# Moving the causal mask from TensorE to GpSimd and reordering TensorE's turn in the last stage of a four-block kernel

## The reference

```
log_d = lf[..., 1:, None] - lf[..., None, 1:] + i_pre[..., None, :]
log_d = jnp.where(mask, log_d, -jnp.inf)          # mask: t >= s
m = jnp.max(log_d, axis=-1, keepdims=True)
d_mat = jnp.exp(log_d - m)
s_mat = (q @ k.T) / sqrt(32) * d_mat
denom = max(abs(sum(s_mat)), exp(-m)) + 5e-5
h = s_mat @ v / denom                             # 8 heads of 32
h = h * rsqrt(mean(h * h) + 1e-6) * gain;  x = x + h
gate = softmax(ln(x) @ gate_w.T)                  # 8 experts
t = ln(x) @ lora_U                                # 16 ranks each
x = x + ln(x) @ weight.T + (gate * t) @ lora_V / 16
```

## Time and profile before

| | us |
|---|---|
| median of 3 runs (466.28 to 468.68) | 466.73 |
| the profiled execution | 466.06 |
| its span, first to last instruction | 464.3 |
| PE busy | 357.2 (77%) |
| DVE busy | 347.6 (75%) |
| ACT busy | 246.8 (53%) |
| POOL busy | 214.6 (46%) |
| last stage, from its first log_d to the end | 347.2 to 464.3 |

### The profile page before, as it was taken

The page is one execution under the profiler, slowest core; times in us unless marked ns, Lnnn a source line. Parts: engine busy times, 40 slices in busy tenths (PEclk is TensorE's granted clock), DMA queues, the critical chain, the costliest instruction groups (busy, mean ns, idle before and its releaser), DMA issues.

```text
span 464.3 us, 9131 instructions
## 1 busy us (share of the span) xinstructions
PE 357.2 (77%) x3130; PEld 252.2 (54%) x3137; DVE 347.6 (75%) x998; ACT 246.8 (53%) x454; POOL 214.6 (46%) x215
## 2 busy tenths in 40 slices
PE   3986789998896999434566777657658999999965
PEld 2775567776674777212444444435445666666522
DVE  3887647789999788778999999996243777777751
ACT  1563345654442455444757575757435666666530
POOL 1115001146767463168676767676102555444430
PEclk9998899999996999856878887897958999999985
DMA  7599999966473520000000000000001122222000
GB/s 226 154 259 288 282 339 261 215 145 120 80 146 61 107 32 1 1 0 2 0 0 2 0 1 0 1 1 0 2 0 18 30 47 47 47 47 48 23 24 24
DMA packets 48046, 35.79 MB, mean 77 GB/s; under 512 B 20096, under 2 KB 44032, under 8 KB 47872
## 3 DMA queue, kind: packets, MB, share of 16 engines
q1 hardware_dynamic: 48000, 35.20, 31.6%
HBM read 26.80 MB, written 8.39 MB: 76 GB/s over the span
## 4 chain that ended last, share of the span: by engine, by line
PE 46%; DVE 28%; issue 12%; ACT 5%; DMA 3%; SPq 3%; POOL 1%; DVEq 0%; ACTq 0%
DVE ve L725 6%; PE PS L1436 5%; DVE sm L733 4%; PE PS L1225 3%; PE PS L1214 3%; PE PS L1426 3%; PE PS L1283 3%; PE PS L1244 3%; PE PS L1205 3%; PE PS L1204 3%; PE PS L1403 2%; DVE sm L711 2%; DMA scr_k<-kpart 2%; PE PS L1421 2%; SPq L315 2%
## 5 line engine op out<-in xcount | busy, mean ns | idle before, releaser
L991 ACT ACTIVATE pT<-PS 128x512 f32<-128x512 f32 x64 | 36.5, 596 | 58.6 <-PE PS L1205 58.4
L606 DVE TENSOR_REDUCE negm<-PS 128x4 bf16<-128x512 f32 x64 | 42.3, 683 | 13.3 <-PE PS L1214 13.2
L1318 PE MATMUL PS<-identf,w2f 128*128 128x128 f32 x128 | 23.4, 341 | 36.4 <-ACT w2f L1042 36.4
L469 POOL TENSOR_TENSOR kst<-kst,rows 128x1024 f32<-128x1024 f32 x16 | 37.6, 2349 | 29.6 <-ACT kst L1053 29.6
L453 POOL TENSOR_TENSOR sm<-sm,mhalf 128x1 f32<-128x1 f32 x16 | 11.4, 713 | 81.6 <-DVE sm L638 81.6
L1318 PEld LDWEIGHTS PS<-identf,w2f 128*128 128x128 f32 x128 | 18.3, 174 | 40.8 <-ACT w2f L1042 34.9
L483 POOL TENSOR_TENSOR kst<-kst,rows 128x1024 f32<-128x1024 f32 x16 | 37.7, 2359 | 0.0
L1205 PE MATMUL PS<-identb,negm 128*128 128x128 bf16 x256 | 35.6, 222 | 0.0
L1042 ACT ACTIVATE w2f<-kst,sm 128x1024 f32<-128x1024 f32 x16 | 18.4, 1149 | 31.2 <-DVE sm L741 31.0
L1225 PE MATMUL PS<-pT,vx 128*32 128x128 f32 x512 | 27.7, 291 | 5.0 <-ACT pT L991 4.9
L725 DVE TENSOR_SCALAR ve<-mv 128x2 f32<-128x2 f32 x20 | 30.1, 1504 | 1.8
(11 more groups left out here) (225 smaller groups left out, 1073.2 us busy)
## 6 DMA issues: line engine op xcount, KB each, us to landing
scr_q<-qpart SPq DMA_DIRECT2D x8, 384.0 KB, 5.0
scr_k<-kpart SPq DMA_DIRECT2D x8, 384.0 KB, 6.1
rows<-in_rows SPq DMA_DIRECT2D x1, 2056.0 KB, 11.6
X<-in_x SPq DMA_DIRECT2D x8, 256.0 KB, 4.8
CTXT<-in_ctxT SPq DMA_DIRECT2D x8, 256.0 KB, 4.5
cTb<-in_ctxT SPq DMA_DIRECT2D x16, 128.0 KB, 4.3
vx<-in_ctx SPq DMA_DIRECT2D x16, 128.0 KB, 2.8
out<-rest SPq DMA_DIRECT2D x16, 128.0 KB, 1.7
```

Of the source, the lines that this page charges most:

```text
L469: gp.tensor_tensor(n2[q.slot], n2[q.slot], ln2g, ALU.mult).then_inc(b_g2, 1)
L606: v.tensor_reduce(negm[f.slot % 2][:, 4 * hg:4 * hg + 4], PS[:, 2 + hg % 2, :].rearrange("p (h k) -> p h k", h=4), AX_X, ALU.max, negate=T ...
L991: s.activation(pT[:, hg, :], PS[:, hg % 2, :], ACT.Exp, scale=float(DH0) ** -0.5).then_inc(a_e, 1)
L1318: last = t.transpose(PS[:, 5 + i // 4, (i % 4) * 128:(i % 4 + 1) * 128], u2[:, i * 128:(i + 1) * 128], identf[:])
```

## The change

The mask leaves PE: `maskb` and its matmul go, log_d is one `APARTS` matmul that starts the bank and four `MPARTS` matmuls. In its place POOL runs an `affine_select` in place over each half of `dT` (128 x 512, f32) after ACT's exponential, which writes zero above the diagonal; DVE's weights wait for that (`c_k`) and no longer for the exponential (`c_d`). On POOL the select of half 0 stands behind the gain of `b`, that of half 1 behind L503 and L505 of `c` and ahead of `rr` of `b`.

PE's order becomes: scores (`a`), yT transposes (`b`), nd transposes (`e`), log_d(0), gate transpose (`d`, now into bank 1, columns 256 to 384, waiting for exp(1) of `a` and for the copy `xT` of `e`), values (`a`), experts' product (`d`), log_d(1), products (`e`). The orders of DVE, ACT and SP don't change.

```diff
-            step(gp.memset(maskb[:], 0.0))
-            step(gp.affine_select(out=maskb[:], in_=maskb[:], compare_op=ALU.is_ge, fill=-30000.0, base=0,
-                                  pattern=[[1, 128]], channel_multiplier=-1))
...
+                def masked(half):
+                    pool.wait_ge(c_d, n.b * 2 + half + 1)
+                    d3 = dT[half].rearrange("p (j t) -> p j t", j=4)
+                    gp.affine_select(out=d3, in_=d3, compare_op=ALU.is_ge, fill=0.0, base=0,
+                                     pattern=[[0, 4], [1, 128]], channel_multiplier=-1).then_inc(c_k, 1)
...
+                if n:
+                    masked(0)
                 if c:
                     z = smd[c.slot % 2]
...
+                if n:
+                    masked(1)
                 if b:
                     pool.wait_ge(c_ms, b.b + 1)
...
-                    dve.wait_ge(c_d, a.b * 2 + n + 1)
+                    dve.wait_ge(c_k, a.b * 2 + n + 1)
...
-                    s.activation(gtT[:], PS[:, 6, 0:128], ACT.Copy).then_inc(d_gT, 1)
+                    s.activation(gtT[:], PS[:, 1, 256:384], ACT.Copy).then_inc(d_gT, 1)
...
-                    t.matmul(bank, identb[:], maskb[:].unsqueeze(1).to_broadcast([128, 4, 128]), start=True, stop=False)
+                    t.matmul(bank, APARTS[:, n.used, :], rowsel[:, hs:hs + 4].unsqueeze(2).to_broadcast([128, 4, 128]),
+                             start=True, stop=False)
                     for j in range(4):
-                        t.matmul(bank[:, j * 128:(j + 1) * 128], rowsel[:, hs + j:hs + j + 1].to_broadcast([128, 128]),
-                                 MPARTS[:, n.used, :], start=False, stop=False, skip_group_check=True)
-                    t.matmul(bank, APARTS[:, n.used, :], rowsel[:, hs:hs + 4].unsqueeze(2).to_broadcast([128, 4, 128]),
-                             start=False, stop=True).then_inc(c_arg, 1)
+                        last = t.matmul(bank[:, j * 128:(j + 1) * 128], rowsel[:, hs + j:hs + j + 1].to_broadcast([128, 128]),
+                                        MPARTS[:, n.used, :], start=False, stop=(j == 3))
+                    last.then_inc(c_arg, 1)
...
-                if b:
-                    pe.wait_ge(c_yT, b.b + 1)
...
+                if b:
+                    pe.wait_ge(c_yT, b.b + 1)
...
-                if d:
-                    pe.wait_ge(d_g, d.b + 1)
-
-                    pe.wait_ge(c_yT, b.b + 1 if b else NB)
-                    t.transpose(PS[:, 6, 0:128], gt[:], identf[:]).then_inc(d_gt, 1)
                 if n:
                     log_d(0)
                 if d:
-                    pe.wait_ge(d_gT, d.b + 1)
-                    t.matmul(PS[:, 7, 0:D], gtT[:], wlv[:], start=False, stop=True, skip_group_check=True).then_inc(d_l, 1)
+                    pe.wait_ge(d_g, d.b + 1)
+                    exps_read(1)
+                    if e:
+                        pe.wait_ge(d_xT, e.b + 1)
+                    t.transpose(PS[:, 1, 256:384], gt[:], identf[:]).then_inc(d_gt, 1)
                 if a:
                     pe.wait_ge(c_ld[a.slot % 2], 16 * (a.b // 2 + 1))
                     pe.wait_ge(c_sm, a.b * 2 + 2)
+
+                    pe.wait_ge(c_yT, a.b)
...
+                if d:
+                    pe.wait_ge(d_gT, d.b + 1)
+                    t.matmul(PS[:, 7, 0:D], gtT[:], wlv[:], start=False, stop=True, skip_group_check=True).then_inc(d_l, 1)
                 if n:
                     log_d(1)
```

More of the change, by code:

```diff
@@ L123, in build @@
         identf = sb("identf", [128, 128]); identb = sb("identb", [128, 128], BF16)
-        upper = sb("upper", [128, 128]); maskb = sb("maskb", [128, 128], BF16)
+        upper = sb("upper", [128, 128])
         onesf = sb("onesf", [128, 128]); mhalf = sb("mhalf", [128, H1])
@@ L246, in build @@
         c_z = sem("c_zeroed")
-        c_arg = sem("c_log_d_ready"); c_s = sem("c_scores_ready"); c_d = sem("c_d_ready")
+        c_arg = sem("c_log_d_ready"); c_s = sem("c_scores_ready"); c_d = sem("c_d_ready"); c_k = sem("c_d_masked")
         c_sm = sem("c_weights_ready"); c_pv = sem("c_pv_done"); c_yT = sem("c_yT_ready")
@@ L490, in _, with turn_cd @@
                 turn_b(tau, *peeled(tau, NB, 4, 9))
-            def turn_cd(_n, _a, b, c, _e, _d):
+            def turn_cd(n, _a, b, c, _e, _d):
+                def masked(half):
[3 more added lines that the diff above has]
+                                     pattern=[[0, 4], [1, 128]], channel_multiplier=-1).then_inc(c_k, 1)
                 if b:
@@ L1405, in turn_cd @@
                     last.then_inc(c_s, 1)
+                if b:
+                    pe.wait_ge(c_yT, b.b + 1)
+                    exps_read(0)
+                    for i in range(4):
+                        last = t.transpose(PS[:, 0, i * 128:(i + 1) * 128], yTc[:, i * 128:(i + 1) * 128], identf[:])
+                    last.then_inc(c_t4, 1)
                 if e:
```

## The result

The changed kernel takes 482.24 us (median of 4 runs, 480.1 to 485.97), the kernel before 466.50 beside it (465.87 to 468.68): a ratio of 1.034, 95% interval 1.027 to 1.040. It is slower by 15.7 us where 14.6 were forecast, inside the range and of the forecast sign.

What follows compares the result with a forecast made beforehand. PE bounds the kernel before at 5.90 us a turn; after the change a four-engine ring of 7.13 does. 466.06 - 0.9 (first turns) + 13.5 (11 turns) + 1.4 (turn 16) + 0.55 (tail) = 480.6 us, range 471 to 488.

Steps and rivals of the forecast that it cites:

- The ring: Chain from gate exponential through weights, values, experts' product, DVE's queue and nd to the next exponential: 7.13 us a turn.
- the product's place decides: On PE, the experts' product behind the values holds up DVE's queue, 1.4 us later; 11 turns cost +13.5 us.
- PE stays the bound: Rival: DVE's successors need not wait, PE sets the turn and the mask's removal pays: 460.0 us; chance 0.08.
- the gate transpose and the copies have room: In a 7.13 us turn, the gate transpose waits for xT until 1.4 us, done before the values at 2.37.
- PE's work: PE busy about 5.2 us, at most 5.5, of a 7.13 us turn.
- rival of a falling clock: Rival: PE busy 73% of the turn, clock drops, 2.1 us more per such turn; three give 487 us; chance 0.15.
- The mask matmuls buy nothing, the selects cost nothing: In full turns, removing the mask's 0.43 us from PE gains nothing; POOL's selects, 0.55 us each, cost nothing.
- The price at which selects would cost: On POOL in a 7.13 us turn, selects would cost time only at 1.9 us each.
- The first turns: Turns 0 to 4, up to turn 5's exponential: -0.9 us, with POOL's row of work limiting the gain.
- The tail: Gate transpose waits for xT in turns 17 and 19, 0.35 and about 0.2 us: +0.55 us.

Runs made afterwards that it cites:

- e2: Kernel before with only the experts' product moved behind the values: 484.13 us, ratio 1.037, 7.23 us a turn.
- e1: Changed kernel with the experts' product ahead of the values again, behind the gate transpose: 480.94 us, ratio 1.027, 6.84 us a turn.
- e9: Kernel before with only the scores moved ahead of the yT transposes: 472.11 us, ratio 1.011, 6.41 us a turn.
- e10: Kernel before with only the gate transpose moved behind log_d(0), still in bank 6: 472.22 us, ratio 1.013, 6.39 us a turn.
- e4: Changed kernel with the mask back on PE as a matmul and no selects: 483.06 us, ratio 1.035, 7.21 us a turn.
- e5: Changed kernel with each select run twice on POOL: 486.74 us, ratio 1.041, 7.19 us a turn.
- e8: Kernel before, mask on PE, with DVE's output sum put behind the sum into X: 466.46 us, ratio 0.999, 5.91 us a turn.
- e3: Kernel before with only the mask moved to POOL selects, PE's old order: 466.86 us, ratio 1.000, 5.82 us a turn.
- e11: Kernel before with mask as selects, the first select held until the sum into X is done: 466.71 us, ratio 0.998, 5.77 us a turn.
- e7: Kernel before with mask as selects and DVE's output sum put behind the sum into X: 468.89 us, ratio 1.004, 6.10 us a turn.

## Why the prediction was right, and where it was not

- **The ring.** Forecast 7.13 us, measured 7.20. Its terms, forecast and measured: exponential to weights 2.22, 2.20; hop to the values 0.15, 0.10; values 1.09, 1.09; product 0.51, 0.63 (from 407.25 to 407.88); hop 0.03, 0.04; L892 to nd 2.62, 2.63; nd to exponential 0.51, 0.51. One term was mis-sized: 0.51 was the product's share of a stream on PE; behind the values its last matmul's end counts, 0.12 more. Over 12 turns that is 1.4 us, of which the other terms give back 0.6.
- **That the product's place decides** was right (e2), and so was the price of the move. What the text of the forecast left open is what is late next once it is undone. The rival "PE stays the bound" named as its deciding point that the product ends within 0.38 us of the weights; e1 restores the product's place and still has 6.84. So the step of the working that failed is this rival's, that PE would then set the turn at 5.47 us. The forecast's own sentence, that the gate transpose and the copies have room, was said of a turn of 7.13 and holds there; they don't have it in one of 5.9. I costed the new order only inside the ring that I had found, not as a change of its own (e9, e10: 0.5 us a turn each).
- **PE's work.** The prediction had PE busy for 5.2 to 5.5 us of a turn, and its rival of a falling clock starts from 5.2 of 7.13. The rows read 68.83 us in the 11 turns from T5, 6.26 a turn, at a granted clock of 1.00 throughout. Why the recorded time is longer was not taken apart. So the case that the rival priced, PE at 73%, did not arise.
- **The mask matmuls buy nothing, the selects cost nothing**: right in the full turns of the changed kernel (e4, e5). The price at which selects would cost, 1.9 us each, was reached by no run; from e5 it can be estimated at 1.7 us each (1.28 for a select run twice, and half of the 0.77 us left). The select takes 0.64 us, not 0.55: two points of 32 and 128 elements were a thin base for 512.
- **The first turns.** Forecast -0.9, measured +0.4. POOL's row of work was the bound as said, but its neighbours stretch: in turn 3 the gain of `b`, L885, a select and the sum into X ran side by side and took 0.69, 0.83, 0.83 and 0.74 us:

```profile
365.05 0.69 POOL L500 TENSOR_TENSOR hd<-yc,rows 128x256 f32<-128x256 f32 x1
365.19 0.83 DVE L885 TENSOR_TENSOR hd<-hd,rr 128x256 f32<-128x256 f32 x1 [0.98 <-POOL rr L515]
...
365.69 0.83 POOL L494 TENSOR_SCALAR_AFFINE_SELECT lnT<-lnT 128x512 f32<-128x512 f32 x1
...
366.05 0.74 DVE L895 TENSOR_TENSOR X<-hd,X 128x256 f32<-128x256 f32 x1
```

  I had counted one such stretch, L885 beside the gain, and none by the selects. In turn 4 PE then waited 1.95 us for nd, and its next matmuls ran at the lower clock level (L1387 0.63 us, not 0.38). The runs part the gain from the cost: the scores' move alone takes 2.2 us off these turns (e9, 20.29), and the selects put 1.0 on (22.87 with them, 21.83 without in e4).
- **The tail.** Forecast +0.55, measured -1.4. The wait for xT came as forecast: the gate transpose of turn 17 started 1.49 us behind the exponential, 1.05 before. What the forecast left out is the clock, which falls in both tails, but in other turns. The products of turns 17 and 19, first in the kernel before:

```profile
443.40 1.55 PE L1436 MATMUL PS<-wd,xT 128*128 128x392 f32 x4 [0.61 <-DVE rest L885]
455.36 2.95 PE L1436 MATMUL PS<-wd,xT 128*128 128x392 f32 x4 [0.61 <-DVE rest L885]
```

  And of the changed kernel:

```profile
464.84 2.95 PE L1446 MATMUL PS<-wd,xT 128*128 128x392 f32 x4 [0.61 <-DVE rest L892]
477.04 1.55 PE L1446 MATMUL PS<-wd,xT 128*128 128x392 f32 x4 [0.61 <-DVE rest L892]
```

  So turns 17 and 18 are 1.3 us longer in the changed kernel, and what follows is 2.7 us shorter. Over all profiled kernels the tail takes 22.4 to 26.0 us (e8 and e4), with products between 1.55 and 2.95 us. The gain of this one trace is therefore luck. The clock was thought of as a risk of the full turns only; there it stayed at 1.00.
- **The other 4.8 us** of the profiled difference arose ahead of the stage, in code that is the same; the medians (15.7 us apart) hold less of it. What makes that part longer or shorter from run to run was not tried.

Three errors nearly cancelled: 0.9 too little for the ring (14.9 for 15.8), 1.3 too little for the first turns, 2.0 too much for the tail. So 14.6 against 14.8 flatters the working.

## What to carry to other kernels

An engine that is 100% busy is the bound only by the slack of the next ring, the difference between its turn and that ring's: sum the chain from one instruction to the same one a turn later across all engines before counting a removed instruction as gain (here 0.43 us taken from PE were worth 0.08, e3). A wait in an in-order queue costs everything queued behind it, so when a producer moves back, look for where its consumer stands in its own queue. And when several moves each lengthen a different ring, only the longest shows; undo or price them one at a time.

## What the runs showed of the hardware

VectorE operations stretch beside a GpSimd operation, and GpSimd's beside VectorE's. The sum of two SBUF tensors of 128 x 256 took 0.41 us alone, 0.60 partly and 0.82 wholly beside a select (e11, e3, e7); the select 0.64 alone, 0.83 beside such sums; a TENSOR_SCALAR of 128 x 8 went from 0.15 to 0.53 us. The weights of 128 x 512, which read one operand from PSUM, were hardly touched: a pair takes 1.28 us, and 1.34 in a first turn of the changed kernel beside a select. The statistics of 128 x 256 (L910 in e11), with one input, kept their 0.42 us beside a select. The Trainium skill ("GPSIMD Engine Reference", section 8) states the rule, contention with VectorE instructions of two SBUF inputs or in a two-port mode, without a size; the rows of the sums agree with it, and give the size for this kernel. Whether the TENSOR_SCALAR, which has one SBUF input, ran in a two-port mode no row shows. I had drawn on it for a rival and not for the selects that the change itself adds, and e7 is what that cost.
